# Two products of a gated attention stage change places on TensorE

## The chip, the cores and the metric

The kernel runs on one core of a Trainium2 chip. The metric is the device time of one execution in microseconds (us), as the median of several runs. All numbers are float32.

## The reference, cut to what matters

The input is 2048 tokens (32 sequences of 64) of width 256. Six sublayers follow each other, each on a normalised input and added back: cross attention, self attention, a ternary linear layer, a second cross attention, a gated attention unit, and a mixture of 160 experts of which each token takes 8. The change lies in the fifth:

```python
    hid = silu(xn @ W_hidden + b_hidden)          # 256 -> 1024
    v, gate = hid[..., :512], hid[..., 512:]
    qk = silu(xn @ W_qk + b_qk)                   # 256 -> 128
    qk2 = qk[..., None, :] * os_weight + os_bias
    q, k = qk2[..., 0, :], qk2[..., 1, :]
    attn = square(relu(q @ k.T / n))
    out = (attn @ v) * gate
    return out @ W_out + b_out
```

## The kernel before, in words

The tokens are cut into 16 tiles of 128 rows (two sequences each), and the work into three phases. Phase 1 (to about 485 us of the span) does the first two sublayers. Phase 2 (`phase2`, to about 1005 us) does for each tile the ternary layer and the queries of the second cross attention (`stage_c`), its keys and values (`keys_values`), its scores, softmax and mix (`scores`, `softmax`, `mix`), then the gated attention unit (`stage_e`), and the routing to experts (`stage_f`), which hands out places in pages of 64 rows and scatters the rows to them by DMAs of the POOL queue (L773). Behind the last tile `order_pages` makes the table of pages, and phase 3 (`experts`) runs page by page.

Phase 2 is a software pipeline. Each stage is a Python generator that issues instructions between its `yield`s. `weave` sorts all pieces of all tiles by due times written out in `ORDER2`, plus 59.06 for each tile, and so fixes the order of instructions on every engine when the program is built. The due time belongs to the number of the piece and not to what it holds. Each engine works its own instructions in that order; between engines semaphores tell what is done (`done`, `wait`). While `stage_e` of tile j runs, the same engines work on the softmax of tile j+1 and the keys of tile j+2.

The pieces of `stage_e` that matter, for tile j:

- L583, ScalarE: the copy xTE of the normalised, transposed tile.
- L588, TensorE: query and key product, 128 columns, into bank 7. It waits for xTE and for "spot" of tile j-1 (L757 of `stage_f`, VectorE), since the bookkeeping reads bank 7 too. Two calls give four matmuls a tile.
- L592, TensorE: hidden product, 512 columns, into bank 6; also four matmuls a tile. These are the four large products.
- L597 and L598, ScalarE: a copy and a tanh of bank 7 ("qke"). L602 to L605, VectorE: from these the two operands of the scores product.
- L609, VectorE: adds the bias to the hidden product, from bank 6. L620, ScalarE: its tanh. L624, VectorE: the value rows `hid`.
- L614, TensorE: gate products, sixteen matmuls, over bank 7; so they wait for L598.
- L628, TensorE: the scores product. L641 and L645, VectorE: relu and square. L650, TensorE: attention times values.
- L634 and L635, ScalarE: gate activations. L654 and L659, VectorE: gate times attention. L663, TensorE: the output product.

Of the neighbours, L485 on TensorE transposes the exponentials of L472 (ScalarE), and L491 copies the transposes out of their bank (ScalarE, once a tile VectorE). L249 and L268 on ScalarE copy the keys and values. L499 on VectorE and L505 on POOL make the factors of the softmax. L457 is the scores product of the cross attention.

Of the kernel before, what the change touches and what calls it, by code (L numbers as in the profile page):

```python
# [272 lines left out]
def phase2(nc, a, turns, keys_values, routes, rings, sem, bank, X, XN, ident, small, dchain, pool_waits, resident, kT, vv, qs, qb, bg2, sc):  # L273
# [3 lines left out]
    pe, dve, act, pool, sp = nc.tensor, nc.vector, nc.scalar, nc.gpsimd, nc.sync  # L277
    ph = ExitStack()
    with ph:
        def sb(name, shape, dt=F32):  # L280
            return ph.enter_context(nc.sbuf_tensor(name, shape, dt))
# [27 lines left out]
        xTE = sb("xTE", [P, 2, P])  # L309
# [59 lines left out]
        C, D, E, F, R, G, H = turns  # L369
# [179 lines left out]
        def stage_e(j):  # L549
# [27 lines left out]
            for c in range(2):  # L577
                last = pe.transpose(bank[6][:, c * P:(c + 1) * P], xnE[:, 1, c * P:(c + 1) * P], ident[:, :])
# [4 lines left out]
            E.done(j, "act", act.copy(xTE[:, :, :], halves(bank[6])), "xT")  # L583
            yield
            E.wait(pe, "xT", j)
            R.wait(pe, "spot", j - 1)
            for c in range(2):
                last = pe.matmul(bank[7][:, 0:P], wqk[:, c, :], xTE[:, c, :], start=(c == 0), stop=(c == 1))  # L588
            E.done(j, "pe", last, "qk")
            yield  # L590
            for c in range(2):
                last = pe.matmul(bank[6][:, :], xTE[:, c, :], wh[:, c, 0:512], start=(c == 0), stop=(c == 1))  # L592
            E.done(j, "pe", last, "h")
            yield
            E.wait(act, "qk", j)
            E.wait(act, "qk2", j - 1)
# [15 lines left out]
            for c4 in range(4):  # L612
                for c in range(2):
                    last = pe.matmul(bank[7][:, c4 * P:(c4 + 1) * P], wh[:, c, 512 + c4 * P:512 + (c4 + 1) * P], xTE[:, c, :],  # L614
                                     start=(c == 0), stop=(c == 1))
# [16 lines left out]
            for c4 in range(4):  # L632
                src = bank[7][:, c4 * P:(c4 + 1) * P]
                act.activation(gu[:, c4, :], src, ACT.Identity, bias=bg[:, c4:c4 + 1])  # L634
                last = act.activation(gt[:, c4, :], src, ACT.Tanh, bias=bg2[:, c4:c4 + 1], scale=0.5)  # L635
# [3 lines left out]
            for b in range(2):  # L639
                r = slice(64 * b, 64 * b + 64)  # L640
                last = dve.tensor_scalar(rel[r, r], bank[6][r, r], 1.0 / SEQ, 0.0, ALU.mult, ALU.max)  # L641
# [7 lines left out]
            for c4 in range(4):  # L649
                last = pe.matmul(bank[6][:, c4 * P:(c4 + 1) * P], hid[:, c4 * P:(c4 + 1) * P], att[:, :], start=True, stop=True)  # L650
# [11 lines left out]
            for c in range(4):  # L662
                last = pe.matmul(bank[6][:, 0:DIM], og[:, c * P:(c + 1) * P], wout[:, c, :], start=(c == 0), stop=(c == 3))  # L663
# [234 lines left out]
        for i in range(TILES):  # L898
            at = i * PERIOD2
            parts += [(at, f"scores{m}", scores(i, m)) for m in range(2)] + [(at, f"softmax{u}", softmax(i, u)) for u in range(8)]  # L900
            if i:
                parts.append((at, "keys_values", keys_values(i)))
            parts += [(at, p.__name__, p(i)) for p in (stage_c, mix, stage_e, stage_f, count_pages)]
# [1046 lines left out]
```

How the kernel before makes its waits and increments, by code:

```python
    def link(self, ins):  # L99
        self.n += 1
        ins.then_inc(self.sem, 1)
        self.eng.wait_ge(self.sem, self.n)
# [99 lines left out]
    def wait(self, eng, events, i):  # L202
        if i >= 0:
            e, k = max(self.at.get(event, ("pe", 1)) for event in ([events] if isinstance(events, str) else events))
            eng.wait_ge(self.sem[e], i * self.per[e] + k)
# [23 lines left out]
    def keys_values(i, banks_free=None):  # L229
        z = i % 2
        yield
        G.wait(sp, "v3", i - 2)
        sp.dma_start(cT[z][:, :, :], a["ctx2"][i]).then_inc(s_ctx[z], 16)
        yield
        pe.wait_ge(s_ctx[z], (i // 2 + 1) * 16)
        if i == 0:
            banks_free()
        for m in range(2):
# [34 lines left out]
def phase2(nc, a, turns, keys_values, routes, rings, sem, bank, X, XN, ident, small, dchain, pool_waits, resident, kT, vv, qs, qb, bg2, sc):  # L273
# [74 lines left out]
            pool.memset(xw[z][:, :, DIM:WIDE], 0.0).then_inc(s_set, 1)  # L348
        last_row = pool.to_reg(ROWS - 1)
        pe.transpose(bank[6][0:1, 0:P], sc[:, 7:8], ident[:, :]).then_inc(s_max, 1)
        dve.memset(ones_e[:, :], 1.0).then_inc(s_set, 1)
        dve.memset(lift[:, :], -1.0).then_inc(s_set, 1)
        dve.wait_ge(s_max, 1)
        dve.tensor_reduce(sc[0:1, 3:4], bank[6][0:1, 0:P], AX.X, ALU.max).then_inc(s_max, 1)
        pe.wait_ge(s_max, 2)
        pe.matmul(bank[7][:, 0:1], ones[0:1, 0, :], sc[0:1, 3:4], start=True, stop=True).then_inc(s_max, 1)
        dve.wait_ge(s_max, 3)
        link(dve.tensor_copy(sc[:, 2:3], bank[7][:, 0:1]))
```

## Time and profile before

| | |
|---|---|
| median of 3 runs | 1386.85 us (1385.37 to 1387.29) |
| the profiled execution's own time | 1384.27 us |
| its span, first to last instruction | 1381.1 us |
| TensorE (PE) busy | 1244.3 us, 90% |
| VectorE (DVE) busy | 946.3 us, 69% |
| ScalarE (ACT) busy | 605.4 us, 44% |
| GpSimd (POOL) busy | 548.0 us, 40% |
| mean granted TensorE clock | 0.954 of full speed |

The profile names an instruction by its engine and its line in the kernel. PE is the matmul side of TensorE and PEld its weight loads, which run beside the matmuls. Times are microseconds from the start of the span. An arrow `<-` ahead of an engine names what ended the idle time in front of an instruction; between names of tiles it separates what is written from what is read.

### The profile page before, as it was taken

How to read it: one execution, taken by the hardware profiler on the slowest of the kernel's cores; microseconds unless marked ns; L12 is line 12 of the kernel's file. 1: busy time of each engine (PE TensorE's matmuls, PEld its weight loads, DVE VectorE, ACT ScalarE, POOL GpSimd, SP SyncE). 2: the span in 40 equal slices, each digit the busy share in tenths (PEclk: the TensorE clock that was granted, in tenths of full speed). 3: DMA queues.
4: the chain of work that ended last, by engine and by line, in shares of the span. 5: the costliest groups of instructions: out<-in, count | busy, mean ns of one | idle time of the engine just before them, and what ended most of it. 6: DMA issues, size and time to landing. Idle time of an engine off the chain costs nothing.

```text
span 1381.1 us, 34814 instructions
## 1 busy us (share of the span) xinstructions
PE 1244.3 (90%) x11693; PEld 897.9 (65%) x11693; DVE 946.3 (69%) x2728; ACT 605.4 (44%) x1761; POOL 548.0 (40%) x717
## 2 busy tenths in 40 slices
PE   5999999999998689999999999997848999999946
PEld 3667667767766356767776767775636776667725
DVE  2477666666666436787778887777637777777737
ACT  2445555455454156667667677665301111111140
POOL 1011110101100101556666666656616776667730
PEclk8999999999999779999999999999979999999969
DMA  9322323233323000111122111113298899898659
GB/s 308 99 98 90 133 91 138 93 133 108 133 80 106 32 16 16 37 65 53 57 64 73 57 65 54 64 38 103 91 263 254 257 267 279 262 265 253 207 211 368
DMA packets 124879, 185.73 MB, mean 134 GB/s; under 512 B 23285, under 2 KB 90516, under 8 KB 122784
## 3 DMA queue, kind: packets, MB, share of 16 engines
q10 hardware_dynamic: 57376, 77.19, 17.6%
q1 hardware_dynamic: 51200, 71.66, 16.9%
q0 software_dynamic: 16128, 34.67, 7.1%
q8 instruction: 95, 1.56, 0.5%
q14 instruction: 80, 0.66, 0.1%
HBM read 190.88 MB, written 78.25 MB: 195 GB/s over the span
## 4 chain that ended last, share of the span: by engine, by line
PE 43%; ACT 5%; ACTq 5%; DMA 4%; DVE 4%; issue 4%; POOL 1%; SPq 0%; DVEq 0%; POOLq 0%
PE bank L1038 5%; PE bank L1063 5%; PE bank L485 4%; ACT ex L472 3%; PE bank L1023 3%; PE bank L457 3%; ACTq L951 2%; PE bank L663 2%; PE bank L525 2%; PE bank L592 2%; PE bank L614 2%; PE bank L240 2%; PE bank L256 2%; PE bank L1050 1%; PE bank L433 1%
## 5 line engine op out<-in xcount | busy, mean ns | idle before, releaser
L1073 POOL DMA_INDIRECT y_d<-y,xg x208 | 204.0, 981 | 121.1 <-DVE y L1069 85.2
L1043 ACT ACTIVATE ex<-bank 128x256 f32<-128x256 f32 x104 | 40.0, 384 | 278.6 <-PE bank L1038 118.3
L773 POOL DMA_INDIRECT xs_d<-xw,slot_id x128 | 134.3, 1049 | 30.2 <-issue 29.3
L472 ACT ACTIVATE ex<-bank,nmC 128x256 f32<-128x256 f32 x256 | 119.2, 483 | 14.2 <-DVE nmC L466 13.8
L1069 DVE COPY y<-bank 128x512 f32<-128x512 f32 x104 | 71.9, 691 | 70.5 <-PE bank L1063 63.4
L485 PE MATMUL bank<-ident,ex 128*128 128x128 f32 x512 | 79.2, 284 | 20.0 <-ACT ex L472 16.6
L485 PEld LDWEIGHTS bank<-ident,ex 128*128 128x128 f32 x512 | 61.8, 145 | 54.3 <-ACT ex L472 21.1
L1023 PE MATMUL bank<-ident,xg 128*128 128x128 f32 x416 | 70.0, 292 | 19.4 <-DMA xg<-xs_d 19.4
L466 DVE TENSOR_REDUCE nmC<-bank 128x2 f32<-128x512 f32 x128 | 82.8, 680 | 5.7 <-PE bank L457 4.8
L1337 POOL TENSOR_TENSOR stB<-stB,small 128x1 f32<-128x1 f32 x32 | 20.3, 634 | 165.3 <-DVE stB L1334 165.3
L1027 DVE COPY ex<-bank 128x512 f32<-128x512 f32 x104 | 71.5, 687 | 21.0 <-PE bank L1023 16.3
L1023 PEld LDWEIGHTS bank<-ident,xg 128*128 128x128 f32 x416 | 44.7, 143 | 59.3 <-issue 49.1
L1711 POOL COPY recxB<-recB 128x128 f32<-128x128 f32 x32 | 8.4, 293 | 184.9 <-DVE recB L1706 184.9
L1491 ACT ACTIVATE sm<-sm,nm 128x256 f32<-128x256 f32 x128 | 63.5, 499 | 34.3 <-DVE nm L1483 34.2
L491 ACT COPY pTC<-bank 128x512 f32<-128x512 f32 x112 | 65.1, 596 | 19.7 <-PE bank L485 19.5
L1364 PE MATMUL bank<-cT,wk0a 128*128 128x512 f32 x128 | 63.8, 623 | 3.6 <-DVE nm L1483 3.6
L457 PE MATMUL bank<-kTC,qxC 32*128 32x256 f32 x512 | 58.6, 431 | 6.1 <-ACT ex L472 3.3
L505 POOL TENSOR_TENSOR recx<-recC,half 128x128 f32<-128x128 f32 x64 | 24.6, 414 | 89.6 <-DVE recC L499 89.6
L1395 PE MATMUL bank<-pTA,ctxA 128*128 128x512 f32 x128 | 59.1, 605 | 0.8 <-DVE pTA L1511 0.4
L472 ACT ACTIVATION_READ_ACCUMULATOR ex<-bank,nmC 128x1 f32 x256 | 54.5, 213 | 0.0
L1483 DVE CUSTOM_DVE_ANT_0 sm<-bank,mb 128x256 f32<-128x256 f32 x128 | 49.2, 422 | 3.4
L457 PEld LDWEIGHTS bank<-kTC,qxC 32*128 32x128 f32 x512 | 34.2, 194 | 25.7 <-ACT ex L472 13.4
(393 smaller groups left out, 3314.1 us busy)
## 6 DMA issues: line engine op xcount, KB each, us to landing
xs_d<-zeros ACTq DMA_DIRECT2D x16, 1768.0 KB, 7.4
pTC<-in_wexp ACTq DMA_DIRECT2D x104, 256.0 KB
xg<-xs_d SPq DMA_DIRECT2D x310, 68.0 KB
cT<-in_ctx SPq DMA_DIRECT2D x32, 512.0 KB, 4.0
wh<-in_wexp ACTq DMA_DIRECT2D x52, 256.0 KB
cT<-in_wexp ACTq DMA_DIRECT2D x52, 256.0 KB
kTC<-in_wexp ACTq DMA_DIRECT2D x52, 256.0 KB
vvC<-in_wexp ACTq DMA_DIRECT2D x52, 256.0 KB
```

What stands on the lines that cost most here:

```text
L457: last = pe.matmul(bank[hp][:, 256 * b:256 * b + 256], qx[z][rows, m, b, :, :].rearrange("p h t -> p (h t)"), kT[z][rows, m, 256 * b:256 * ...
L466: D.done(i, "dve", dve.tensor_reduce(nm[:, u, :], bank[hp][:, :].rearrange("p (b n) -> p b n", b=2), AX.X, ALU.max, negate=True), f"m{u}")
L472: last = act.activation(ex[:, u, 256 * b:256 * b + 256], bank[hp][:, 256 * b:256 * b + 256], ACT.Exp, bias=nm[:, u, b:b + 1], accum_out=su ...
L485: last = pe.transpose(bk[:, q * P:(q + 1) * P], ex[:, u, q * P:(q + 1) * P], ident[:, :])
L491: D.done(i, en, copy(pT[:, u, :], bk[:, :]), f"pT{u}e")
L773: pool.indirect_dma_start(out=xs_d, out_offset=bass.IndirectOffsetOnAxis(ap=slot_id[z][:, k:k + 1], axis=0), in_=xw[z][:, k, :], in_offset ...
L1023: last = pe.transpose(bk[:, (2 * c + g) * P:(2 * c + g + 1) * P], xg[:, d % FETCHED, g, c * P:(c + 1) * P], ident[:, :])
L1027: T.done("dve", dve.tensor_copy(xgT[d % HELD], bk[:, :]))
L1038: last = pe.matmul(bk[half * PAGE:(half + 1) * PAGE, g * P:(g + 1) * P], xgT[d % HELD][:, at:at + PAGE], w[d % RING_W * 4 + 2 * g + half][ ...
L1063: last = pe.matmul(bk[half * PAGE:(half + 1) * PAGE, g * DIM:(g + 1) * DIM], hs[d % HELD][:, at:at + PAGE], w[d % RING_W * 4 + 2 * g + hal ...
L1069: D.done("dve", dve.tensor_copy(y[:, n, :, :].rearrange("p g n -> p (g n)"), bk[:, :]))
L1073: pool.indirect_dma_start(out=y_d, out_offset=bass.IndirectOffsetOnAxis(ap=who, axis=0), in_=y[:, n, g, :], in_offset=None, bounds_check=l ...
```

## The change

The pieces of L588 and L592 change places. The wait for xTE stays ahead of both; the wait for "spot" goes with L588. The sum of pieces and all due times stay.

```diff
             E.wait(pe, "xT", j)
+            for c in range(2):
+                last = pe.matmul(bank[6][:, :], xTE[:, c, :], wh[:, c, 0:512], start=(c == 0), stop=(c == 1))
+            E.done(j, "pe", last, "h")
+            yield
             R.wait(pe, "spot", j - 1)
             for c in range(2):
                 last = pe.matmul(bank[7][:, 0:P], wqk[:, c, :], xTE[:, c, :], start=(c == 0), stop=(c == 1))
             E.done(j, "pe", last, "qk")
-            yield
-            for c in range(2):
-                last = pe.matmul(bank[6][:, :], xTE[:, c, :], wh[:, c, 0:512], start=(c == 0), stop=(c == 1))
-            E.done(j, "pe", last, "h")
             yield
             E.wait(act, "qk", j)
```

## Rows read from the trace of the kernel before

**Rows 1.** The page: the chain that ended last, by engine and by line.
```profile
PE 43%; ACT 5%; ACTq 5%; DMA 4%; DVE 4%; issue 4%; POOL 1%; SPq 0%; DVEq 0%; POOLq 0%
PE bank L1038 5%; PE bank L1063 5%; PE bank L485 4%; ACT ex L472 3%; PE bank L1023 3%; PE bank L457 3%; ACTq L951 2%; PE bank L663 2%; PE bank L525 2%; PE bank L592 2%; PE bank L614 2%; PE bank L240 2%; PE bank L256 2%; PE bank L1050 1%; PE bank L433 1%
```

**Rows 2.** The chain in order of time, at L592: start, us, what.
```profile
561.32 1.72 PE bank L592 x4
591.88 1.72 PE bank L592 x4
620.96 1.72 PE bank L592 x4
...
916.18 1.72 PE bank L592 x4
```

**Rows 3.** Timeline of TensorE in one tile: start, us, instruction [idle time before].
```profile
591.27 0.61 PE L588 MATMUL bank<-xTE,wqk 128*128 128x128 f32 x4
591.72 1.88 PE L592 MATMUL bank<-wh,xTE 128*128 128x512 f32 x4
593.44 1.04 PE L485 MATMUL bank<-ident,ex 128*128 128x128 f32 x8
...
599.36 1.06 PE L650 MATMUL bank<-att,hid 128*128 128x128 f32 x8
```

**Rows 4.** Timeline of ScalarE in that tile.
```profile
592.22 0.40 ACT L598 ACTIVATE qk<-bank,bqk 128x128 f32<-128x128 f32 x1
...
594.08 1.07 ACT L491 COPY pTC<-bank 128x512 f32<-128x512 f32 x2 [0.55 <-PE bank L485]
...
605.54 1.07 ACT L268 COPY vvC<-bank 128x512 f32<-128x512 f32 x2 [5.08 <-PE bank L262]
```

**Rows 5.** Timelines of VectorE and POOL in that tile.
```profile
592.71 0.29 DVE L602 SCALAR_TENSOR_TENSOR qk<-qk 128x128 f32<-128x128 f32 x1
...
597.45 1.06 DVE L645 TENSOR_TENSOR att<-rel 128x128 f32<-128x128 f32 x1
...
594.53 1.48 POOL L505 TENSOR_TENSOR recx<-recC,half 128x128 f32<-128x128 f32 x4 [5.22 <-DVE recC L499]
```

**Rows 6.** Timelines of weight loads and ScalarE: L614's load, and one that waited.
```profile
594.21 0.53 PEld L614 LDWEIGHTS bank<-xTE,wh 128*128 128x128 f32 x4
...
942.79 0.38 ACT L583 COPY xTE<-bank 128x256 f32<-128x256 f32 x1
...
943.22 0.52 PEld L588 LDWEIGHTS bank<-xTE,wqk 128*128 128x128 f32 x4 [0.75 <-ACT xTE L583]
```

**Rows 7.** Timelines of TensorE, ScalarE and VectorE in the last tile.
```profile
966.85 1.20 PE L588 MATMUL bank<-xTE,wqk 128*128 128x128 f32 x4 [3.64 <-DVE spot L757]
967.83 3.62 PE L592 MATMUL bank<-wh,xTE 128*128 128x512 f32 x4
971.25 2.42 PE L614 MATMUL bank<-xTE,wh 128*128 128x128 f32 x16
...
968.34 0.36 ACT L598 ACTIVATE qk<-bank,bqk 128x128 f32<-128x128 f32 x1
...
973.70 0.37 ACT L634 ACTIVATE gu<-bank,bg 128x128 f32<-128x128 f32 x1 [0.86 <-PE bank L614]
...
971.49 0.69 DVE L609 TENSOR_TENSOR hid<-bank,bh 128x512 f32<-128x512 f32 x1 [1.11 <-PE bank L592]
```

**Rows 8.** Timeline of TensorE: the wait of L485 in two tiles.
```profile
757.54 0.66 PE L485 MATMUL bank<-ident,ex 128*128 128x128 f32 x4 [0.99 <-ACT ex L472]
...
846.26 0.66 PE L485 MATMUL bank<-ident,ex 128*128 128x128 f32 x4 [0.99 <-ACT ex L472]
```

**Rows 9.** Stretches: us, busy us (instructions) of each engine, clock, DMA share, GB/s.
```profile
583.10:586.51 3.41, 3.41 (x15) 3.23 (x15) 2.58 (x6) 2.24 (x9) 3.04 (x4) 0.50 0.15 46
...
760.60:764.01 3.41, 3.41 (x16) 3.37 (x15) 2.64 (x6) 2.31 (x10) 3.04 (x4) 0.50 0.14 43
849.35:852.76 3.41, 3.41 (x25) 2.83 (x24) 3.31 (x9) 2.34 (x10) 3.05 (x4) 1.00 0.15 46
```

## The prediction

> **What bounds the kernel now.** I read the page first, then the chain of waits through the changed stage, then the engines' timelines of one tile, then the tiles that differ from it. The chain has TensorE as its largest owner and the hidden projection of L592 in it [rows 1]. Inside the changed stretch it runs through L592 in every tile up to the last but one: thirteen pieces of the same length from 561.32 to 916.18, of which three are shown [rows 2]. The reader should see there that a tile takes 29.08 us (591.88 to 620.96) or 30.56 us (561.32 to 591.88). Of these twelve distances four are long, so a long tile costs 1.48 us more. The timeline of TensorE shows why the chain stays on it: from L588 to L650 one group follows the other without idle time [rows 3]. So in this stage a delay on VectorE or ScalarE counts only if it reaches TensorE, and one that does is kept, because nothing further on has room to give it back: the next wait, L485 on ScalarE's exponential, is 0.99 us in every tile and moves with TensorE [rows 8].
>
> **What the change does to TensorE's own work.** Nothing is added or taken away. Per tile four matmuls of L588 and four of L592 change places; they are neighbours before (L588 from 591.27, L592 from 591.72, transposes of L485 from 593.44) and no other TensorE group stands between them [rows 3]. Their sum of time is the same, so TensorE is at the transposes at 593.44 as before. No DMA moves, and SP and POOL get nothing new. What moves is when the two results are ready: the hidden product 0.45 us earlier, the query and key product 1.72 us later, the length of L592's piece [rows 2].
>
> **Who is glad of the earlier one.** Nobody in a full tile: its reader, the addition of L609, stands behind L602 to L605 in VectorE's order, and those wait for the late product.
>
> **Who is hurt by the later one.** L588's product now ends at about 593.60 (where L592's did). In the last tile, where ScalarE also stood waiting for it, L598 ended 0.65 us after L588 (968.05 to 968.70) [rows 7]. By that the tanh is ready at 594.25 in place of 592.62 [rows 4]. Behind the waiting L597 stand, on ScalarE, one softmax exponential, two copies of transposes, a key copy, L620, a copy and the gate activations. They start 1.63 us later at first, and idle time gives some back: the pair of copies waited 0.55 us for TensorE anyway [rows 4]. So the copies and L620 come about 1.0 us late, and the rest is made up before L268, where ScalarE idles 5.08 us [rows 4]. On VectorE L602 moves from 592.71 by the same 1.63 us; L624, which waits for L620, and L645 behind it come 1.0 us late, L645 near 598.45 in place of 597.45 [rows 5]. On POOL the product L505 starts up to 1.63 us later and has 5.22 us of idle time ahead of it [rows 5].
>
> Now where each of these meets TensorE. (1) L614, the gate products, waits for the tanh because it writes over the same bank. Its first weights load at 594.21 now, right behind the transposes [rows 6]. A waiting load started 0.05 us after its releaser: L583 ended at 943.17, the load of L588 began at 943.22 [rows 6]. With the tanh ready at 594.25 the load begins at 594.30: **0.1 us late in each tile** (0.09, rounded up as all these ends are to 0.01). Bounds: nothing, if the load or the matmul behind it catches up, since only the start is late and the weights are small; 0.2 us if ScalarE and the two hand-overs take 0.1 us longer than there. I take 0.1, the nearest row. (2) L650 needs L645. L650 starts at 599.36, and L645 with its 1.06 us would end at 599.51 [rows 3, 5]. That is a long one for 128x128 elements: it lies beside POOL's arithmetic behind L505, which moves further than L645 does. I count nothing; if it stays so long the price is 0.2 us more in such a tile. (3) The other meetings (transposes, scores product, mix) have 0.4 us or more and cost nothing; were the cover of (3) gone, the whole 1.63 us would show.
>
> Fifteen tiles pay 0.1 us: 1.5 us.
>
> The Trainium skill (TensorE: Matmul & The Clock Gate, "Step-by-step: what each phase is for") says that TensorE pulls weight loads ahead of matmuls in flight. Read broadly that makes the stall of (1) nothing, and the sum 2.0 us below before (rival B) in place of the one below. The two loads of [rows 6] speak for a wait that holds the load too.
>
> **The last tile** is another matter. There L588 waits 3.64 us for L757 (the page bookkeeping of the tile before), with L592 behind it, and the granted clock is low, so that L592 takes 3.62 us [rows 7]. The new order puts L592 in front of that wait. Its reader L609 no longer waits the 1.11 us for it; L609 would end near 971.1 in place of 972.18, and L620, 0.7 us on, near 971.8. The gate activations then start near 971.7 in place of 973.70, since L614 no longer has L592 ahead of it: from L588's end at 968.05, 0.65 us for the tanh and at most its 2.42 us, part of it at the low clock, give 971.2 [rows 7]. **Gain 2.0 us**, once. Late next are the gate activations themselves, then L659 and the output product. From there the chain goes through the routing to the page table and the expert stage, so the gain is kept. Bounds: 1.1 us (only L609's wait) to 3.6 us (the whole wait).
>
> **The clock.** This is the term that decides. A long tile holds a stretch at 1.2 GHz: the granted clock is 0.50 of full in the stretches from 583.10 and 760.60, which begin twice 88.75 us apart, and full in the one from 849.35, once more 88.75 us on [rows 9]. Two plain tiles and a long one make 88.7 us: the kernel keeps step with the chip. Each fall follows the thin place of a tile, the 0.99 us idle ahead of L485; all tiles have it, and only some fall. The thin place at 757.54 is 3.06 us ahead of 760.60 and falls; that at 846.26 is 3.09 us ahead of 849.35 and does not [rows 8, 9]. So the falls sit on an edge, and a thin place that comes later against this beat is on the side that falls. Adding 0.1 us to a tile moves it that way by 0.1 us each tile, several times the 0.03 us that separate the two. How wide the falling side is no row tells; the bounds are no long tile more and ten more (all fourteen). I take five more, the middle: 5 x 1.48 = 7.4 us. Were the thin place to pass across to the far side, the four long tiles could also vanish: -5.9 us.
>
> The same page ("Why this matters for your kernels") names only far longer idle gaps as the cause of a slow clock; by that rule a gap of 1 us never costs, and the sum would be +1.5 - 2.0 = -0.5 us (rival A). The measured falls behind 0.99 us already speak against it.
>
> **Sum** against the profiled execution's 1384.27 us: +1.5 - 2.0 + 7.4 = +6.9, so 1391.2 us. The median of the runs, 1386.85, lies 2.6 us above that execution. If that is one or two long tiles more, as I assume (no row shows it), they are mostly among the five; I go 0.8 us up and predict 1392 us.
>
> **Rivals.**
> A. The stall is real and the number of long tiles stays: 1386.85 + 1.5 - 2.0 = 1386.4. For it: runs of before agree within 2 us, so the beat is stable. Against: 0.03 us decides between a fall and none.
> B. The stall does not exist because the weights load anyway: 1386.85 - 2.0 = 1384.9, with full tiles of 29.08 us. Against: [rows 6].
> C, the other side: fewer long tiles. Place: the thin place ahead of L485. Price 1.48 us a tile, up to four. It decides once the added time per tile carries the thin place beyond the falling side: 1386.85 - 0.5 - 5.9 = 1380.5. For it: nothing but the unknown width.
> D. The 1.63 us on ScalarE and VectorE reach TensorE in full tiles, through L650 or the copies: up to 15 x 1.63 = 24.5, less 2.0, so 1409.4, or 1393 if a third gets through. Against: the slack listed in (1) to (3).
>
> **How the numbers follow.** Forecast 0.50, A 0.24, B 0.10, C 0.08, D 0.08. A measurement of this kernel can tell 0.2% (2.8 us) from no change. The forecast and D are slower, save a small part of the forecast with one or two more long tiles; A is the same, with some on either side; B is mostly the same; C is faster. That gives 0.58 slower, 0.31 same, 0.11 faster. The range for 8 in 10 runs from 1384.3, which takes in A and half of B, to 1398.
>
> **What would show it.** L614's first weight load 0.1 us behind the transposes, with ScalarE's L598 named as the releaser, and plain tiles of 29.18 us: step (1). ScalarE idle some 1.5 us ahead of L597: the late product. L650 without idle time ahead of it: step (2). In the last tile L592 right behind L583, and about 2 us less from L578 to L663. More tiles near 30.7 us than four: the clock term; the granted clock over the stage falls with them. The prediction is wrong if full tiles stay at 29.08 us, if their long ones stay at four or fewer, or if any idle time on TensorE of over 0.3 us appears between L588 and L663.

## The result and the profile after

| | before | after |
|---|---|---|
| median of the runs, us | 1386.11 (1384.57 to 1391.13, 6 runs) | 1396.75 (1393.59 to 1398.91, 6 runs) |
| profiled execution, us | 1384.27 | 1398.48 |
| span, us | 1381.1 | 1395.8 |
| mean granted TensorE clock | 0.954 | 0.947 |

After takes 1.0076 times the time of before, with a 95% interval of 1.0056 to 1.0096: slower by 10.6 us, where 1392 was predicted. In the kernel after, L587 is the hidden product and L592 the query and key product; from L597 on the line numbers are those of before.

The page says that nobody does more work than before:

```profile
span 1395.8 us, 34799 instructions
PE 1255.3 (90%) x11693; PEld 907.6 (65%) x11693; DVE 945.3 (68%) x2728; ACT 603.5 (43%) x1761; POOL 549.4 (39%) x717
```

VectorE, ScalarE and POOL are busy as long as they were. TensorE is busy 11 us longer for the same work, which points at its clock. The chain in order of time, at the hidden product (start, us, what), answers to [rows 2]:

```profile
559.27 1.72 PE bank L587 x4
589.95 1.72 PE bank L587 x4
620.62 1.72 PE bank L587 x4
...
927.33 1.72 PE bank L587 x4
```

There are again thirteen such pieces, so twelve distances, one for each tile. Before, eight were 29.06 to 29.09 us (plain tiles) and four 30.56 (long tiles). Now all twelve are 30.66 to 30.68 (589.95 to 620.62 is 30.67): each tile is a long one, and 0.11 us longer than the long ones were. The stretches at the low clock, with the columns of [rows 9]:

```profile
611.85:615.26 3.41, 3.41 (x16) 2.73 (x12) 2.95 (x6) 1.67 (x7) 2.87 (x5) 0.50 0.13 41
642.57:645.98 3.41, 3.41 (x17) 2.76 (x13) 2.92 (x6) 1.75 (x7) 2.89 (x4) 0.50 0.13 41
673.29:676.70 3.41, 3.41 (x17) 2.76 (x13) 2.87 (x6) 1.80 (x8) 2.93 (x4) 0.50 0.13 41
```

There are twelve of them from 581.13 to 919.05, one in every tile, and each begins 30.72 us behind the one before. Before, the records had them at 583.10, 671.85, 760.60 and 907.37. Over the whole stage, from 555 to 925 us, first before and then after:

```profile
555.00:925.00 370.00, 353.21 (x2892) 268.75 (x2894) 296.18 (x820) 251.63 (x798) 227.93 (x311) 0.98 0.17 58
```

```profile
555.00:925.00 370.00, 353.19 (x2793) 269.94 (x2792) 285.89 (x792) 239.22 (x765) 222.13 (x299) 0.94 0.17 57
```

TensorE is busy for the same 353.2 us and does 99 instructions less in them. That is how the slower clock looks here: the busy share doesn't move, while the count under it falls.

One full tile on TensorE, to be held against [rows 3]:

```profile
651.13 1.88 PE L587 MATMUL bank<-wh,xTE 128*128 128x512 f32 x4
652.85 0.61 PE L592 MATMUL bank<-xTE,wqk 128*128 128x128 f32 x4
653.29 1.04 PE L485 MATMUL bank<-ident,ex 128*128 128x128 f32 x8
654.17 2.05 PE L614 MATMUL bank<-xTE,wh 128*128 128x128 f32 x16
...
659.32 1.06 PE L650 MATMUL bank<-att,hid 128*128 128x128 f32 x8
```

L614 follows the transposes without a printed wait, but takes 2.05 us. The row sums sixteen matmuls, and a gap of 0.1 us within the sum is not shown as idle time. Before, in the tile of [rows 3], it took 1.95:

```profile
594.31 1.95 PE L614 MATMUL bank<-xTE,wh 128*128 128x128 f32 x16
```

The weight loads show the delay itself:

```profile
654.17 1.86 PEld L614 LDWEIGHTS bank<-xTE,wh 128*128 128x128 f32 x16
```

They begin 3.04 us behind the start of the two products (651.13); before it was 2.94 (591.27 to 594.21, [rows 3, 6]). The tanh below ends at 654.12, 0.05 us ahead of the load. ScalarE in that tile, against [rows 4], and VectorE, against [rows 5]:

```profile
653.49 0.37 ACT L597 ACTIVATE qk<-bank,bqk 128x128 f32<-128x128 f32 x1 [1.55 <-PE bank L592]
653.76 0.36 ACT L598 ACTIVATE qk<-bank,bqk 128x128 f32<-128x128 f32 x1
...
665.50 1.07 ACT L268 COPY vvC<-bank 128x512 f32<-128x512 f32 x2 [4.79 <-PE bank L262]
```

```profile
654.22 0.29 DVE L602 SCALAR_TENSOR_TENSOR qk<-qk 128x128 f32<-128x128 f32 x1 [1.68 <-issue]
...
658.38 0.29 DVE L645 TENSOR_TENSOR att<-rel 128x128 f32<-128x128 f32 x1
```

ScalarE waits 1.55 us for the late product, and L268, whose idle time was 5.08 us, still has 4.79: the delay has been absorbed. The last tile, against [rows 7]:

```profile
974.64 0.38 PE L578 MATMUL bank<-ident,xnE 128*128 128x128 f32 x2
975.49 1.98 PE L587 MATMUL bank<-wh,xTE 128*128 128x512 f32 x4 [0.46 <-ACT xTE L583]
978.58 0.71 PE L592 MATMUL bank<-xTE,wqk 128*128 128x128 f32 x4 [1.11 <-DVE spot L757]
980.00 3.37 PE L614 MATMUL bank<-xTE,wh 128*128 128x128 f32 x16 [0.72 <-ACT qk L598]
...
987.09 1.99 PE L663 MATMUL bank<-wout,og 128*128 128x256 f32 x8 [0.54 <-DVE og L659]
```

The wait for the page bookkeeping falls from 3.64 to 1.11 us, since the hidden product now fills it, and L578 to L663 takes 12.45 us. Before it took 14.56:

```profile
962.82 0.38 PE L578 MATMUL bank<-ident,xnE 128*128 128x128 f32 x2
...
977.38 1.99 PE L663 MATMUL bank<-wout,og 128*128 128x256 f32 x8 [1.02 <-DVE og L659]
```

The difference of the two profiled spans, 14.7 us, by stretches between the same instructions:

| stretch | before | after | difference |
|---|---|---|---|
| start to the first L578 | 527.02 | 525.56 | -1.46 |
| first L578 to that of tile 14 | 412.40 | 425.56 | +13.16 |
| to that of tile 15 | 23.39 | 23.52 | +0.13 |
| last tile, L578 to L663 | 14.56 | 12.45 | -2.11 |
| to the end of the page table | 27.93 | 28.16 | +0.23 |
| expert stage | 375.8 | 380.5 | +4.7 |

The second row is eight more long tiles (8 x 1.48 = 11.8) and fourteen times 0.1. The last row need not be the change's: a second profile of the kernel before (one run, 1384.43 us) has 378.8 us there, and those of the experiments on such chips lie between 378.1 and 384.6. By the medians the account closes without it and without the first row: 11.8 + 1.5 - 2.1 = 11.2, against 10.6 measured.

### The profile page after: what moved, and what is told of

The parts are those of the page before. It is cut to its first block, busy times and chain, and to the rows that moved or that the text cites. A ratio compares the mean times of both kernels' runs of the same rounds, so it can differ in the third digit from the quotient of the medians.

```text
span 1395.8 us, 34799 instructions
## 1 busy us (share of the span) xinstructions
PE 1255.3 (90%) x11693; PEld 907.6 (65%) x11693; DVE 945.3 (68%) x2728; ACT 603.5 (43%) x1761; POOL 549.4 (39%) x717
## 4 chain that ended last, share of the span: by engine, by line
PE 39%; ACTq 8%; ACT 6%; issue 5%; DVE 4%; DMA 3%; POOL 1%; SPq 0%; DVEq 0%; POOLq 0%
ACTq L951 4%; PE bank L485 4%; PE bank L1038 4%; ACT ex L472 3%; PE bank L1063 3%; PE bank L457 3%; PE bank L614 2%; ACTq L991 2%; PE bank L663 2%; PE bank L525 2%; PE bank L1023 2%; PE bank L587 2%; PE bank L256 2%; PE bank L240 2%; ACTq L945 2%
## 5 line engine op out<-in xcount | busy, mean ns | idle before, releaser
L485 PE MATMUL bank<-ident,ex 128*128 128x128 f32 x512 | 81.9, 291 | 20.6 <-ACT ex L472 17.2
L485 PEld LDWEIGHTS bank<-ident,ex 128*128 128x128 f32 x512 | 63.9, 150 | 46.7 <-ACT ex L472 21.4
```

The source lines that it names most:

```text
L485: last = pe.transpose(bk[:, q * P:(q + 1) * P], ex[:, u, q * P:(q + 1) * P], ident[:, :])
```

## The experiments

Some words first. A fall is the start of a stretch at the low clock; a tile that holds one is a long tile. The thin place is the 0.99 us in which TensorE waits for ScalarE's exponential ahead of L485. The theory: a late tanh adds 0.1 us to each tile, and this shift alone makes the tiles keep step with the falls, so that tile after tile meets one, at 1.48 us a tile (the lock). Rivals: that the late product itself costs (on ScalarE or VectorE), that the new order of TensorE's work is what lowers the clock, or that the number of long tiles is chance.

**The 0.1 us without the new order.** pad1 is the kernel before with one idle transpose in each tile (idle: nobody reads its result), into the bank that the query and key product then overwrites.

```diff
             R.wait(pe, "spot", j - 1)
+            for n in range(1):
+                pe.transpose(bank[7][:, 0:P], xTE[:, 0, :], ident[:, :])
             for c in range(2):
```

> The order of before, with one more transpose on TensorE ahead of L588 in every tile (written over at once by L588's own product): 0.11 us of work, nothing late on ScalarE or VectorE. Theory (added time shifts the tile against the beat of the clock): tiles of 30.67 us from about the second on, some 12 long ones in place of 4; time about 1.5 + 8 x 1.48 = 13 us over before, so 1397 to 1400 (no gain in the last tile). Rival 1 (the clock falls because of the new order, its late tanh and the shifted work of ScalarE): plain tiles of 29.18 us, 4 or 5 long ones, 1388. Rival 2 (the number of long tiles is chance and differs from program to program): anything between.

Measured: 1397.69 us (1396.82 to 1404.07, 6 runs) beside 1386.52 for the kernel before there, 1.0094 (1.0064 to 1.0123). Its chain:

```profile
653.79 1.72 PE bank L594 x4
684.47 1.72 PE bank L594 x4
...
745.82 1.72 PE bank L594 x4
775.00 1.72 PE bank L594 x4
804.18 1.72 PE bank L594 x4
```

Ten of the twelve tiles are 30.67 or 30.68 us, two (745.82 to 804.18) 29.18. So 0.11 us of plain work, in the old order and with an early tanh, is enough for the lock. The sum closes: 16 x 0.11 and six more long tiles at 1.48 make 10.6, and 11.2 was measured. Nor is it chance: the mean granted clock of the six runs is 0.944 to 0.946, that of the 29 runs of the kernel before beside them 0.948 to 0.956.

**Where a fall comes.** The traces show this directly. Take the distance from the end of the thin place to the start of the low stretch; in the kernel after, for the tile that starts at 651.13, it is 673.29 - 670.64 = 2.65 us (the first line stands in the section above, the second with fill_after below). In the stretch of twelve tiles:

| kernel | tiles that fell: distances in order, us | no fall at, us |
|---|---|---|
| before | 2.99; 3.02; 3.06; 2.96 | 3.15, 3.18, 3.21, 3.09 |
| before, second profile | 2.83, 2.99; 3.04; 2.95 | 3.15, 3.20, 3.08, 3.11 |
| after | 2.52, 2.56, 2.61, 2.65, 2.70, 2.74, 2.79, 2.84, 2.88, 2.93, 2.98, 3.04 | |
| pad1 | 2.83, 2.88, 2.92, 2.97, 3.01, 3.06; 2.77, 2.81, 2.85, 2.89 | 3.10 |

The last column has tiles that kept step and did not fall: its distance goes to the place 30.72 or 88.75 us behind an earlier fall, the two spacings met so far, where the next was due and did not come. (The other plain tiles stand over 4 us ahead of such a place.) In these four profiles 3.06 falls and 3.08 does not. Now the lock can be read. A long tile of 30.67 us adds only 0.05 to the distance of the next (30.72 - 30.67), so tile after tile falls until 3.08 is reached. A long tile of the kernel before has 30.56 and adds 0.16: after one fall, or two, it is out. How many fall also depends on where the twelve tiles come in (2.52 in after, 2.83 in pad1), and what sets that is not shown.

**The new order without the 0.1 us.** In tanh_of_copy the tanh reads ScalarE's copy in SBUF in place of the bank, so the gate products that write over the bank wait for the copy alone.

```diff
-            act.activation(qk[:, 1, :], bank[7][:, 0:P], ACT.Identity, bias=bqk[:, 0:1], scale=0.5)
-            E.done(j, "act", act.activation(qk[:, 0, :], bank[7][:, 0:P], ACT.Tanh, bias=bqk[:, 0:1], scale=0.5), "qke")
+            E.done(j, "act", act.activation(qk[:, 1, :], bank[7][:, 0:P], ACT.Identity, bias=bqk[:, 0:1], scale=0.5), "qkc")
+            E.wait(act, "qkc", j)
+            E.done(j, "act", act.activation(qk[:, 0, :], qk[:, 1, :], ACT.Tanh), "qke")
...
-            E.wait(pe, "qke", j)
+            E.wait(pe, "qkc", j)
```

> The changed order, but the tanh of L598 reads the copy that L597 made, and L614 waits only for that copy, so bank 7 is free 0.26 us earlier. Theory: L614's load has no stall, TensorE's tiles are 29.08 and 30.56 us with 4 to 6 long ones, and with the gain of the last tile the time is 1384. Rival 1 (the new order as such makes the falls): tiles of 30.6 us stay in the majority, 1395.

Measured: 1383.62 us (1380.91 to 1389.33, 12 runs), 0.9983 (0.9965 to 1.0001), 13 us below after. TensorE, its weight loads, ScalarE and the chain:

```profile
651.27 1.88 PE L587 MATMUL bank<-wh,xTE 128*128 128x512 f32 x4
...
654.31 1.95 PE L615 MATMUL bank<-xTE,wh 128*128 128x128 f32 x16
```

```profile
654.20 1.87 PEld L615 LDWEIGHTS bank<-xTE,wh 128*128 128x128 f32 x16
```

```profile
653.63 0.37 ACT L597 ACTIVATE qk<-bank,bqk 128x128 f32<-128x128 f32 x1 [1.55 <-PE bank L592]
654.03 0.31 ACT L599 ACTIVATE qk<-qk 128x128 f32<-128x128 f32 x1
```

```profile
562.75 1.72 PE bank L587 x4
591.82 1.72 PE bank L587 x4
620.88 1.72 PE bank L587 x4
651.43 1.72 PE bank L587 x4
```

ScalarE waits the same 1.55 us and the tanh is later than in after by its distance to L597 (0.40 against 0.27), yet the gate products take 1.95 us again, their loads begin 2.93 us behind the two products in place of 3.04, and plain tiles have 29.07; three of twelve are long. So what cost 0.1 us was the bank that came free late, and not the late operands of the scores product.

**Filling the thin place.** fill_after is the changed kernel with two idle products (four matmuls) in the first thirteen tiles, behind the routing logits, in the thin place [rows 8].

```diff
             F.done(j, "pe", last, "lg")
+            if j < TILES - 3:
+                for n in range(2):
+                    pe.matmul(bank[6][:, 0:DIM], ident[:, :], xfT[:, :, :].rearrange("p c n -> p (c n)"), start=True, stop=True)
             yield
```

> The changed kernel, with two more calls (four matmuls of 256 columns, 0.86 us) in tiles 0 to 12 in the thin place, behind L713 and ahead of the waiting L485, into a bank that is free there; they lie in the 0.99 us idle. The stall of 0.1 us stays. Theory: no low stretch between 550 and 940 us, all tiles 29.18 us, so 12 x 1.48 = 17.8 us less than the changed kernel: about 1379. Rival 1 (the falls come from elsewhere in the tile): the long tiles stay, 1397. Rival 3 (TensorE's extra time is mostly waits that the clock only seems to cause): tiles above 29.3 us at full clock.

Measured: 1384.7 us (1379.82 to 1389.25, 12 runs), 0.9994 (0.9975 to 1.0014). TensorE, first in the kernel after and then here:

```profile
670.64 0.66 PE L485 MATMUL bank<-ident,ex 128*128 128x128 f32 x4 [1.00 <-ACT ex L472]
```

```profile
578.68 1.03 PE L717 MATMUL bank<-xfT,ident 128*128 128x256 f32 x4
579.84 0.66 PE L485 MATMUL bank<-ident,ex 128*128 128x128 f32 x4
```

```profile
555.00:925.00 370.00, 363.54 (x3007) 274.46 (x3006) 296.93 (x827) 249.83 (x798) 229.73 (x313) 1.00 0.17 58
```

The idle products fill all but 0.13 us of the 1.00, the clock is full over the whole stage, and all twelve distances are 29.17 to 29.19 us, with the 0.1 us of the stall still in them. So without the thin place there is no fall. Its chain spans 350.20 us over the twelve tiles against 368.06 in after, but the run is 5.7 us slower than expected: 17.9 us went in, 12 came out. The profiles say where some of it went. The page table is complete at 1000.30 against 1015.25, so 15.0 of the 17.9 reach it: behind the twelve tiles, where no idle products stand, the clock is low for 6.83 us from 930.62, and in after it is not. The expert stage takes 382.7 us against 380.5; what lengthens it is open.

**The last tile.** swap_last has the new order in the last tile only; swap_but_last_b in all others (the same edit with `j < TILES - 1`).

```diff
+            hidden_first = j == TILES - 1
+            qk_is, h_is = ("second", "first") if hidden_first else ("first", "second")
+            for n in range(2):
+                if (n == 0) == hidden_first:
+                    for c in range(2):
+                        last = pe.matmul(bank[6][:, :], xTE[:, c, :], wh[:, c, 0:512], start=(c == 0), stop=(c == 1))
+                else:
+                    R.wait(pe, "spot", j - 1)
+                    for c in range(2):
+                        last = pe.matmul(bank[7][:, 0:P], wqk[:, c, :], xTE[:, c, :], start=(c == 0), stop=(c == 1))
+                E.done(j, "pe", last, ("first", "second")[n])
...
```

Left out are the old lines, the `yield`s, and the waits of ScalarE (`qk_is`) and VectorE (`h_is`).

> The order of before in tiles 0 to 14, the changed one in the last tile alone. Theory: full tiles as before (29.08 and 30.56 us, 4 to 6 long ones); the last tile gives 2.1 us from L578 to L663; 1384 against 1386. Rival (the gain of the last tile is lost again in the page table or the expert stage): no difference, 1386.

> As swap_but_last, again. On the other chip the first run had plain and long tiles of 29.17 and 30.67 us, eight of them long. If before takes 1386 here: 10 to 12 long ones and 1398, 2 us over the changed kernel.

Measured: swap_last 1382.71 us (1380.66 to 1386.24, 12 runs), 0.9976 (0.9960 to 0.9993); swap_but_last_b 1395.4 (1391.37 to 1400.28, 12 runs) beside 1387.6, 1.0057 (1.0037 to 1.0076). The last tile of swap_last:

```profile
964.29 0.38 PE L578 MATMUL bank<-ident,xnE 128*128 128x128 f32 x2
965.14 1.98 PE L591 MATMUL bank<-wh,xTE 128*128 128x512 f32 x4 [0.46 <-ACT xTE L583]
...
976.69 2.00 PE L668 MATMUL bank<-wout,og 128*128 128x256 f32 x8 [0.48 <-DVE og L664]
```

That is 12.40 us, with tiles of 29.08 and 30.56 as before (five of twelve long). swap_but_last_b has 14.40 us there and ten of twelve tiles long. So by the profiles the two parts of the change separate: the last tile gives 2.1 us, the others take the rest, and swap_last is the fastest order of the three. The medians agree in sign and not in size. swap_but_last_b was expected at 1398, 2 us over after, and lies 1.35 under it; its 7.8 us over before and swap_last's 3.8 us under make 4.0 where the whole change cost 10.6. Ten long tiles in place of twelve explain 3.0 of the 6.6 that are missing; the rest is open.

**More than 0.1 us.** pad3_b has three idle transposes in the place of one.

> As pad3, again, since the first went to a chip on which the kernel before takes 1497 us. If before takes 1386 here, the theory (length of the tile against the beat) expects 7 to 10 long tiles of 14 and 1396 to 1399, no more than pad1; eight times the added work would be 1420.

Measured: 1408.28 us (1403.85 to 1409.36, 6 runs), 1.0138 (1.0109 to 1.0166), a miss by 9 us or more. Stretches and chain:

```profile
583.17:586.58 3.41, 3.41 (x19) 2.61 (x16) 3.04 (x6) 1.32 (x6) 2.92 (x4) 0.50 0.16 49
613.89:620.72 6.83, 6.83 (x32) 6.03 (x33) 5.30 (x13) 3.20 (x12) 5.67 (x7) 0.50 0.17 61
```

```profile
592.98 1.72 PE bank L594 x4
625.53 1.72 PE bank L594 x4
654.93 1.72 PE bank L594 x4
684.34 1.72 PE bank L594 x4
715.24 1.72 PE bank L594 x4
```

Plain tiles have 29.40 us and long ones 30.90, and two have 32.53 and 32.55 (the latter from 592.98 to 625.53), with a low stretch of 6.83 us. The number of falls does not simply grow with the added time: eight tiles fall where pad1 has ten, but two of them for twice as long. The distances tell which: those of single length came at 2.30, 2.92, 2.74, 2.57, 2.39 and 2.21 us, the two double ones at 2.12 and 2.03. Here a long tile is longer than the 30.72 between two falls, so the distance shrinks by 0.18 a tile until a fall comes double. That fits these two cases and was not tried further.

The twelve tiles take 368.08 us, 13.2 more than before; by the expectation's own terms it would be about 10. The rest of the miss is elsewhere: the table is complete at 1022.79 against 1005.3, and the expert stage takes 384.6 us, the longest on such chips.

**Both gains together.** fill_swap_last_b has swap_last's last tile and the idle products.

> As fill_swap_last, again. On the other chip no stretch of low clock lay between 550 and 930 us, but a wait of VectorE at L535 made tiles of 30.1 us. If before takes 1386 here: all tiles 29.08 us; 1376 if the 7.4 us of swap_last's five long tiles all show, 1381 to 1384 if the expert stage gives 5 us back, as after fill_after's filled tiles.

Measured: 1384.39 us (1379.27 to 1390.94, 12 runs), 0.9978 (0.9958 to 0.9998). All its tiles are 29.07 to 29.09 us, and the page table is complete at 998.74, 5.9 us before swap_last's 1004.63. Nothing of that is left in the median: 1382.71 / 1386.52 is 0.9973 and 1384.39 / 1387.6 is 0.9977. Its profile shows 381.5 us of expert stage against 378.3, so 3.2 of the 5.9 us are given back there. Since fill_after does likewise, an earlier table seems worth less than its time; one profile of each is too little to call that shown.

**Another chip.** Three of these edits also ran on a chip on which the kernel before takes 1496.73 us (1491.92 to 1504.27, 24 runs).

> As pad1, with three more transposes a tile (0.33 us) in place of one. Theory (the tile's length against the beat of the clock decides): plain tiles of 29.40 us; the thin place moves through the falling side three times as fast, so long tiles come in shorter runs, 7 to 10 of 14; time 16 x 0.33 + about 4 x 1.48 = 11 us over before, 1396 to 1399, no more than pad1 with a third of the work. Rival 4 (each bit of work costs about eight times its length, as pad1 seems to say): three times pad1's 11 us, 1420. Rival 1 (work alone costs its length): 1392.

> The changed order in tiles 0 to 14, that of before in the last tile. Theory: 10 to 12 long tiles of 30.67 us and no gain in the last one: 2.1 us over the changed kernel, 1398 to 1399. Rival (the last tile's new order has a part in the loss): at or under the changed kernel, 1396.

> The order of before in tiles 0 to 14, the changed one in the last, and the two extra calls of fill_after in tiles 0 to 12. Theory: all tiles 29.08 us, no low stretch from 550 to 930 us. Against swap_last this takes away 5 x 1.48 = 7.4 us of phase 2, against fill_after 1.5 us. If all of it shows: 1376. Rival 5 (fill_after's time, 5 us above what its tiles promise, says that the expert stage gives time back when phase 2 is shorter or filled): 1381 to 1384, with the stretch from the page table to the end 3 to 6 us longer than in before.

Measured: pad3 1500.55 us, 1.0022 (1.0001 to 1.0042); swap_but_last 1489.15, 0.9956 (0.9931 to 0.9980); fill_swap_last 1488.02, 0.9944 (0.9922 to 0.9966). The expectations fail here: pad3 costs 3.8 us and not 11, the new order in all but the last tile makes the kernel faster, and in fill_swap_last no tile of the twelve falls, as expected, but they take 29.4 to 30.1 us in place of 29.08. The tiles are different before any edit. In one profile of the kernel before on that chip (1502.1 us), nine of the twelve tiles fall, one of them for 6.83 us, VectorE waits 2.8 us at L535 in four, and tiles take 29.1 to 33.1 us. In swap_but_last seven fall, that wait of 2.8 us comes once, and tiles have 29.17 and 30.67 us but for one of 30.24. So there the edit takes falls away, where on the other chips it adds them. The expert stage takes 466 to 469 us. Why L535 waits there is open, and each of these is one profile; the runs neither support nor refute the lock. They do show that the sign of the new order in tiles 0 to 14 is not the same on every chip. The changed kernel itself did not run there.

## Why the prediction was right, and where its size was off

The kernel got slower by the mechanism forecast, and the time lies in the range. By its steps:

- **TensorE's own work, the same:** right. L587 to L650 follow one another without a wait, as in [rows 3].
- **The tanh 1.63 us later, absorbed behind it:** right. ScalarE idles 1.55 us at L597 (some 1.5 predicted), L650 has no idle time ahead of it, and L268 keeps 4.79 us. L645 costs 0.29 us in this tile in place of 1.06, so step (2), feared at 0.2 us, had more room than the sum gave it. The row chosen was the exception: of the thirteen L645 of that stretch before, the median is 0.29 and 1.06 the longest.
- **L614 0.1 us late in each tile:** right. L614's group takes 2.05 us, its first load begins 0.1 us later behind the two products, tiles are 0.11 longer, and tanh_of_copy removes just that. Rival B (no stall) falls with it: the load began 0.05 us behind the end of the tanh, so it was held by that wait. The Trainium skill (TensorE: Matmul & The Clock Gate, "Step-by-step: what each phase is for") has weight loads pulled ahead of matmuls in flight; here that did not carry the load past a wait.
- **The last tile, -2.0 us:** right, at -2.11, and swap_last has 12.40 us there by itself. Counted from L578, L609 comes 1.2 us earlier and the gate activations 2.1 (1.1 and 2.0 forecast). Part of the gain is the clock: before, the hidden product took 3.62 us at the low clock behind the wait, now 1.98 us at the full clock ahead of it. In tanh_of_copy, with the same order, the clock is low for 6.83 us from 974.20, and the tile takes 13.23 us.
- **The clock, five more long tiles at 1.48, +7.4:** the mechanism is right and the term was mis-sized. It was eight more, all twelve of the stretch, at the price predicted: 11.8 us. Five was the middle between two bounds and had no row behind it. What it missed is the length of the long tile itself: 30.67 us is within 0.05 of the 30.72 between two falls, where 30.56 was 0.16 off, so a tile that fell put the next at nearly the same distance. The edge was read rightly from one pair of thin places (3.06 falls, 3.09 does not), and so was the side: a later thin place falls. How wide that side is could not be read before; falls come down to 2.52 us in after and to 2.03 in pad3_b. That it was twelve of twelve, and not the ten of pad1, is in part the luck of where the execution came in.
- **The 0.8 us added to the sum:** the reason given, one or two long tiles more in the typical run of before than in the profiled one, is not borne out: a second profile has four of twelve again, at other places. The addition is small beside the term above. The medians of before on such chips lie within 1386.1 to 1387.6.

Rival A (the number of long tiles stays, 1386.4) is refuted by the chain. C (1380.5) did not happen, though its premise did elsewhere: without falls the twelve tiles take 4.7 us less than before (350.20 against 354.86), but fill_after shows no gain over before in the median. D (the 1.63 us reach TensorE) is refuted by tanh_of_copy, where ScalarE is as late and nothing is lost.

The ledger lets the sum be redone with the measured number: +1.5 - 2.1 + 11.8 = +11.2 on 1386.11 gives 1397.3, and 1396.75 was measured.

What stays open: the traces give the distances at which a thin place of 0.99 us makes the clock fall and at which not, but no reason for them, and not what sets the distance at the first tile. Open too are the medians of the two parts that don't add up, and what the expert stage does with an earlier table.

## What to carry to other kernels

Where a loop keeps TensorE nearly full, look at the starts of the low-clock stretches and at the distances of one instruction of the loop. If both have nearly the same beat, a shift of 0.1 us per turn can cost several times its length (in pad1, 11.2 us for 1.8 us of work), and an edit must be judged by its plain turns and its count of long turns separately. The length of a long turn against the beat says whether one fall brings the next. Try the cheap way out too, idle matmuls in the thinnest place, in every turn that has one, and count what the stage behind makes of the time. An order that pays only at the end of a loop (here 2.1 us in the last tile) belongs in the last turn alone; and where one reader holds a PSUM bank, let it be the shortest one.

## What the runs showed of the hardware

- The granted clock fell to 1.2 GHz for 3.41 us behind an idle time of only 0.99 us, in a stretch where TensorE is busy 95% of the time (353.19 of 370 us), and no longer fell (1.00 over 370 us) with 0.13 us there. The Trainium skill (TensorE: Matmul & The Clock Gate, "Why this matters for your kernels") names only far longer gaps; here the measurement decides.
- Which thin place was followed by a fall went by its distance to the beat: falls came at 2.03 to 3.06 us behind its end and none where it would have been 3.08 or more (before, its second profile, pad1, after, pad3_b); at 2.12 and 2.03 the low stretch was 6.83 us long.
- A weight load waiting on a semaphore is held with it: L614's load began 0.05 us behind the end of the tanh, 0.1 us late, which cost 0.11 us of a tile and was gone in tanh_of_copy, where the releaser came earlier.
- One kernel, two kinds of chip: the kernel before takes 1386.1 to 1387.6 us on the chips of the main runs, with the expert stage at 375.8 and 378.8, and 1496.73 on another, with 466.1.
